# Layer 1's mixing and projection in one stage

## What is computed

```python
# layer 1, v = _gn(x); x becomes x + relu(res + out)
x_ft = rfft2(v) / sqrt(M * N)
a = x_ft[:, :, :32, :32]
blk1 = einsum('bixy,ioxy->boxy', a, fw1)      # complex, weights differ per mode
blk2 = einsum('bixy,ioxy->boxy', a, fw2)
out_ft[:, :, :32, :32] = blk1
out_ft[:, :, 256 - 32:, :32] = blk2           # row 224 + x of the output is k = -(32 - x)
out = irfft2(out_ft) / sqrt(N * (M // 2 + 1))
res = out @ W + b                             # 64 x 64
```

## Time and profile before

| | us |
|---|---|
| median of 3 runs | 2291.03 |
| lowest and highest run | 2281.13, 2308.48 |
| profiled execution, first to last instruction | 2287.4 |
| TensorE busy in it | 1824.6 |
| VectorE, ScalarE, GpSimd busy | 1462.2, 1128.0, 263.8 |
| mean granted TensorE clock | 0.876 of full speed |
| moved by DMA | 585.68 MB, 256 GB/s |

### The profile page before, as it was taken

One profiled execution on the slowest core, in us unless ns is written; L12 is line 12 of the kernel. 1 busy time (PEld: TensorE's weight loads), 2 busy tenths in 40 slices (PEclk: granted clock), 3 DMA queues, 4 the chain that ended last, 5 costly groups with the idle time before them and its releaser, 6 DMA issues. The chain is left out here.

```text
span 2287.4 us, 57711 instructions
## 1 busy us (share of the span) xinstructions
PE 1824.6 (80%) x24234; PEld 1460.3 (64%) x24234; DVE 1462.2 (64%) x2219; ACT 1128.0 (49%) x1852; POOL 263.8 (12%) x476
## 2 busy tenths in 40 slices
PE   5899989998197433332564999999989999999999
PEld 3677767677155333332553788787868878787887
DVE  5876777773447211112563788787868878787887
ACT  5765556662043000000333677676656767666665
POOL 0000000000102100000252110303021030303000
PEclk9999999999555556655876999999999999999999
DMA  8887887881965999996744888888887888888886
GB/s 302 311 262 239 260 267 255 264 270 23 219 77 110 265 253 284 254 264 172 237 150 133 295 282 289 305 311 321 298 299 271 284 321 296 320 311 319 296 293 261
DMA packets 240450, 585.68 MB, mean 256 GB/s; under 512 B 71170, under 2 KB 160770, under 8 KB 203906
## 3 DMA queue, kind: packets, MB, share of 16 engines
q1 hardware_dynamic: 163778, 515.47, 68.9%
q10 hardware_dynamic: 71040, 60.70, 10.4%
q0 software_dynamic: 5376, 5.76, 0.9%
HBM read 381.01 MB, written 168.30 MB: 240 GB/s over the span
## 5 line engine op out<-in xcount | busy, mean ns | idle before, releaser
L1298 ACT ACTIVATE x_turned<-ps_xt 128x512 f16<-128x512 f32 x512 | 305.6, 597 | 333.2 <-PE ps_xt L1384 333.2
L1428 PE MATMUL ps_y<-apply,x_turned 128*128 128x128 f16 x6144 | 428.5, 220 | 0.0
L1340 DVE TENSOR_TENSOR x_turned<-ps_xt,x_turned 128x512 f16<-128x512 f32 x512 | 351.2, 686 | 106.9 <-ACT x_turned L1298 106.9
L1428 PEld LDWEIGHTS ps_y<-apply,x_turned 128*128 128x128 f16 x6144 | 377.9, 98 | 64.8 <-issue 1.1
L221 DVE TENSOR_TENSOR parts<-stage,parts 128x1024 f16<-128x1024 f32 x256 | 301.9, 1220 | 107.7 <-ACT parts L145 107.1
L1361 DVE SCALAR_TENSOR_TENSOR y_out<-ps_y,relu 128x512 f32<-128x512 f32 x512 | 351.3, 686 | 22.6 <-PE ps_y L1428 4.1
L1384 PE MATMUL ps_xt<-c_eye,x_in 128*128 128x128 f32 x2048 | 312.2, 275 | 22.1 <-DMA x_in<-in_x 22.1
L1308 ACT ACTIVATE relu<-ps_wave 128x512 f32<-128x512 f32 x512 | 303.2, 592 | 13.8 <-PE ps_wave L1414 13.8
L145 ACT ACTIVATE parts<-stage 128x1024 f16<-128x1024 f32 x256 | 255.1, 1049 | 76.3 <-issue 40.7
L1332 DVE SCALAR_TENSOR_TENSOR low_tile<-ps_col,high_tile 128x512 f16<-128x512 f32 x256 | 176.6, 691 | 115.8 <-ACT high_tile L1292 115.8
L290 PE MATMUL row_ps<-parts,c_rows_dft 128*64 128x512 f16 x1536 | 200.6, 389 | 61.5 <-DVE parts L221 53.8
(11 more groups left out here) (121 smaller groups left out, 1978.7 us busy)
## 6 DMA issues: line engine op xcount, KB each, us to landing
stage<-in_x SPq DMA_DIRECT2D x256, 512.0 KB, 4.7
x_in<-in_x SPq DMA_DIRECT2D x128, 1024.0 KB, 9.6
out_y<-y_out SPq DMA_DIRECT2D x128, 1024.0 KB, 6.0
fw_first<-in_fw SPq DMA_DIRECT2D x9, 2048.0 KB, 19.5
fw<-in_fw ACTq DMA_DIRECT2D x8, 2048.0 KB, 22.8
fw<-in_fw SPq DMA_DIRECT2D x8, 2048.0 KB, 20.3
fw_first<-in_fw ACTq DMA_DIRECT2D x7, 2048.0 KB, 20.8
raw<-mixed ACTq DMA_DIRECT2D x12, 1024.0 KB, 7.4
```

What stands on the lines that cost most here:

```text
L1298: nc.scalar.activation(turned[u % 2][:, 0, :, :], ps_turn[u % 2][:, :, :], ACT.Copy).then_inc(turn_high, 1)
L1340: nc.vector.tensor_tensor(v[:, 1, :, :], ps_turn[u % 2][:, :, :], v[:, 0, :, :], ALU.subtract).then_inc(turn_split, 1)
L1428: mm = nc.tensor.matmul(ps_y[u % 2][:, :, 2 * k:2 * k + 2], turned[u % 2][:, p, k, :], apply[:, bass.ds(b, 1), q, :, :].rearrange("p o c w ...
```

## The change

`mixing_1` and `project_1` become one stage, `mix_project`, and `mixed` in memory goes. `norm_0` writes layer 1's modes into `x1`, even rows x in partitions 0 to 63 and odd rows in 64 to 127. fw1 is taken upwards as before, fw2 downwards (`x_of`): the chunk that mixes rows 4c to 4c + 3 of fw1 mixes rows 28 - 4c to 31 - 4c of fw2, which are k = -(4c + 1) to -(4c + 4). So both terms of a k are at hand when its projection comes.

Behind the second pass's step of a row, VectorE's copy (`mixed`, now a tile on the chip) is turned by eight transposes (`turn`), ScalarE copies them out in two pieces (`take_turn`), and `project` multiplies both terms of a k by a table made of W + 1 with the signs of the parts: for each half of the batch four fp32 products (two f, two parts) with 128 stationary columns and 256 moving ones; k = 0 and k = 32 have one f only. ScalarE writes the high part (`take_high`), VectorE the low part (`take_low`). Every eight k the rows are stored to `planes_1`, four DMAs of 256 KiB on SP and four on ScalarE (`store`); this happens in the third step of every second chunk. TensorE's list takes, in each step, projections first, then a turn, then the mixing step. `mixing_1` ran a loop of two chunks; the new lists are written out in full.

The planes of layer 0 and layer 1 are in two arrays now, so an image's planes come in two loads. Image 0's are loaded at the start of `pass_2`, and VectorE and ScalarE relay them in four parts each, between the first column groups, in place of GpSimd during `project_1`. `prepare` goes; VectorE builds the table at the start of `mix_project`. Cut to what is spoken of:

```diff
+def norm_0(nc, B, gram, apply, modes_x, planes_d, x1, fw, fw_first, w):
 ...
-        S_real = m.sb("S_real", [C, 2, K0, B, K0])
+        S_weighted, S_real = (x1[0:C, i * B // 2:(i + 1) * B // 2, :, :, :].rearrange("p b x r y -> p (b x r y)")
+                              .rearrange("p (r x b y) -> p r x b y", r=2, x=K0, b=B) for i in range(2))
 ...
                     for b in range(1, B, 2):
-                        v = xm[0:C, b, :, :, :].rearrange("p x r y -> p (x r y)")
-                        nc.scalar.activation(v, v, ACT.Copy, scale=rstd[0:C, b:b + 1]).then_inc(x1_ready[1], 1)
+                        for odd in range(2):
+                            nc.scalar.activation(x1[odd * C:(odd + 1) * C, b, :, :, :].rearrange("p x r y -> p x (r y)"),
+                                                 xm[0:C, b, odd::2, :, :].rearrange("p x r y -> p x (r y)"), ACT.Copy,
+                                                 scale=rstd[0:C, b:b + 1]).then_inc(x1_ready[1], 1)
 ...
             for b in range(0, B, 2):
-                v = xm[0:C, b, :, :, :].rearrange("p x r y -> p (x r y)")
-                nc.vector.tensor_scalar(v, v, rstd[0:C, b:b + 1], None, ALU.mult).then_inc(x1_ready[0], 1)
+                for odd in range(2):
+                    nc.vector.tensor_scalar(x1[odd * C:(odd + 1) * C, b, :, :, :].rearrange("p x r y -> p x (r y)"),
+                                            xm[0:C, b, odd::2, :, :].rearrange("p x r y -> p x (r y)"), rstd[0:C, b:b + 1],
+                                            None, ALU.mult).then_inc(x1_ready[0], 1)
 ...
+
+    def x_of(f, slot):
+        chunk, k = divmod(slot, KC)
+        return slot if f == 0 else K1 - KC - chunk * KC + k
+
+    def slot_of(f, k):
+        if f == 0:
+            return k
+        chunk = (k - 1) // KC
+        return chunk * KC + chunk * KC + KC - k
+
+    def terms(k):
+        return [f for f in range(2) if f == 0 and k < K1 or f == 1 and k > 0]
+
+    def turn_at(step):
+        chunk, s = divmod(step - KC - 1, CHUNK_STEPS)
+        return chunk * KC + s if 0 <= chunk < CHUNKS_1 and s < KC else None
+
+    def project_at(step):
+
+        chunk, s = divmod(step - KC - 2, CHUNK_STEPS)
+        if not 0 <= chunk < CHUNKS_1:
+            return []
+        return [k for k, at in ((chunk * KC, 0), (chunk * KC + 2, 2), (chunk * KC + 1, 3), (chunk * KC + 3, 4),
+                                (K1 if chunk == CHUNKS_1 - 1 else None, 4)) if at == s and k is not None]
+
+    order = [k for step in range(STEPS + 8) for k in project_at(step)]
 ...
+        weights = [fw_first] + [m.sb(f"fw{i}", [P, OH, KC, 2 * K1]) for i in range(1, SL)]
+        blocks = [m.sb(f"blocks{i}", [P, 2, 2, B, K1]) for i in range(KC)]
+        mixed = [m.sb(f"mixed{i}", [P, MG, 2, C]) for i in range(KC)]
+        T = [m.sb(f"mix_turned{i}", [P, 2, 2, B, K1]) for i in range(KC + 1)]
+        out = [m.sb(f"project_out{i}", [P, 2, 2, 2, 2, FLUSH, C], F16) for i in range(2)]
+        table = m.sb("project_table", [P, 2, 2, 2, 2, C])
 ...
+        def store(eng, blk, h, signal):
+            eng.wait_ge(out_high, rows_done(blk))
+            eng.wait_ge(out_low, rows_done(blk))
+            rows, places = row_pieces(blk, h)
+            for q in range(2):
+                for bh in range(2):
+                    eng.dma_start(planes_1[bh, :, q, :, rows, :].rearrange("p g k c -> p g (k c)"),
+                                  out[blk % 2][:, q, bh, :, h, places, :].rearrange("p g k c -> p g (k c)")
+                                  ).then_inc(signal[blk % 2], 16)
 ...
+            for step in range(STEPS + 8):
+                for blk in flush_at(step):
+                    store(sp, blk, 0, stored)
+                if step % KC == KC - 1 and step // KC + SL < LOADS:
+                    load(sp, 0, step // KC + SL)
 ...
+                        before = slot - KC if slot % KC else slot - 2 * KC
+                        if before >= 0:
+                            act.wait_ge(out_ready, max(number[k] for k in range(K1 + 1) for f in terms(k)
+                                                       if slot_of(f, k) == before) + 1)
+                    y0 = i * MG // 2
+                    nc.scalar.activation(
+                        turned(slot)[:, :, :, :, :].rearrange("p f r b (j g) -> p (f r b) j g", g=MG)[:, :, :, y0:y0 + MG // 2],
+                        ps_turn[i][:, :, :].rearrange("p g (j n) -> p n j g", j=4), ACT.Copy).then_inc(turn_taken, 1)
 ...
+                act.wait_ge(out_ready, number[k] + 1)
+                nc.scalar.activation(out[blk % 2][:, 0, :, :, :, at, :].rearrange("p n g h c -> p (n g h) c"),
+                                     ps_out[number[k] % 2][:, :, :, :, :].rearrange("p n g h c -> p (n g h) c"), ACT.Copy,
+                                     scale=PROJECT_SCALE).then_inc(out_high, 1)
 ...
+            for step in range(STEPS + 8):
+                for k in project_at(step):
+                    take_high(k)
+                for blk in flush_at(step):
+                    store(act, blk, 1, stored_sin)
+                slot = turn_at(step)
+                if slot is not None:
+                    take_turn(slot)
+                if step % KC == KC - 1 and step // KC + SL < LOADS:
+                    load(act, 1, step // KC + SL)
 ...
+            def take_low(k):
+                blk, at = divmod(k, FLUSH)
+                dve.wait_ge(out_high, number[k] + 1)
+                nc.vector.scalar_tensor_tensor(out=out[blk % 2][:, 1, :, :, :, at, :].rearrange("p n g h c -> p (n g h) c"),
+                                               in0=ps_out[number[k] % 2][:, :, :, :, :].rearrange("p n g h c -> p (n g h) c"),
+                                               scalar=PROJECT_SCALE,
+                                               in1=out[blk % 2][:, 0, :, :, :, at, :].rearrange("p n g h c -> p (n g h) c"),
+                                               op0=ALU.mult, op1=ALU.subtract).then_inc(out_low, 1)
+
 ...
+                if part == 0 and chunk >= 1:
+                    dve.wait_ge(turn_ready, 2 * ((chunk - 1) * KC + k + 1))
+                dve.wait_ge(ready, step + 1)
+                nc.vector.tensor_copy(mixed[k][:, :, :, part * OH:(part + 1) * OH].rearrange("p g w o -> p (g w) o"),
+                                      ps[step % BANKS][:, :, :, :].rearrange("p g w o -> p (g w) o")).then_inc(taken, 1)
+                if part == PASSES - 1 and chunk + 1 < CHUNKS_1:
+                    place((chunk + 1) * KC + k)
 ...
+            for step in range(STEPS + 8):
+                for k in project_at(step):
+                    take_low(k)
+                if step < STEPS:
+                    take_mixed(step)
 ...
+                for g in range(MG):
+                    for j in range(4):
+                        y = MG * j + g
+                        last = nc.tensor.matmul(ps[step % BANKS][32 * j:32 * j + R, g, :, :].rearrange("p w o -> p o w"),
+                                                blocks[k][:, :, :, :, y].rearrange("p f r b -> p (f r b)"),
+                                                weights[n % SL][:, :, k, 2 * y:2 * y + 2],
+                                                start=True, stop=True, tile_position=(0, 32 * j))
+                last.then_inc(ready, 1)
 ...
+                chunk, k = divmod(slot, KC)
+                pe.wait_ge(taken, chunk * CHUNK_STEPS + KC + k + 1 + BANKS)
+                for i in range(2):
+                    if slot >= 1:
+                        pe.wait_ge(turn_taken, 2 * (slot - 1) + i + 1)
+                    for g in range(MG // 2):
+                        last = nc.tensor.transpose(ps_turn[i][:, g, :],
+                                                   mixed[k][:, i * MG // 2 + g, :, :].rearrange("p w o -> p (w o)"), w["eye"][:, :])
+                    last.then_inc(turn_ready, 1)
+
+            def project(k):
+                n = number[k]
+                for f in terms(k):
+                    pe.wait_ge(turn_taken, 2 * (slot_of(f, k) + 1))
 ...
+                    pe.wait_ge(out_low, n - 1)
+                for bh in range(2):
+                    pairs = [(f, r) for f in terms(k) for r in range(2)]
+                    for f, r in pairs:
+                        last = nc.tensor.matmul(
+                            ps_out[n % 2][:, bh, :, :, :].rearrange("p g h c -> p (g h c)"),
+                            turned(slot_of(f, k))[:, f, r, bh * HB:(bh + 1) * HB, :].rearrange("p b y -> p (b y)"),
+                            table[:, f, r, :, :, :].rearrange("p g h c -> p (g h c)"), start=((f, r) == pairs[0]),
+                            stop=((f, r) == pairs[-1] and k > 0))
 ...
+            for step in range(STEPS + 8):
+                for k in project_at(step):
+                    project(k)
+                slot = turn_at(step)
+                if slot is not None:
+                    turn(slot)
+                if step < STEPS:
+                    mix(step)
 ...
```

(100 more changed lines are left out.)

440 lines of the change are left out of this document (112 added, 328 removed).

## The result

| | before | changed | forecast |
|---|---|---|---|
| median of 20 runs each (us) | 2290.4 | 2302.3 | 2153 |
| ratio to before, 95% interval | | 1.005 (1.003 to 1.007) | 0.94 |
| span of the profiled execution | 2287.4 | 2305.7 | 2149.8 |
| first column of the last pass starts | 1213.36 | 1103.55 | 1068.7 |
| last pass's first wave product | 1244.0 | 1141.7 | |

The change made the kernel half a per cent slower. The first column comes 110 us earlier, and the last pass, which the change left alone in my sum, gives 121 us back; its column phase takes 7.5 us more, near the forecast (+7). Windows of the changed kernel, columns as in the earlier trace rows: the mixing stage, the stretch between it and the first column, the last pass.

A forecast was written before the change was run, and what follows sets the result against it. The last pass was taken as TensorE's own and unchanged; mixing waited on uneven loads, project_1 left engines idle. First column 144.6 us earlier, less 7 for relay pairs: net -137.6, span 2149.8, plus 3.6 gives 2153 us; 8-in-10 range 2105 to 2225.

The forecast's parts named there:

- forecast (+7): Last pass, first 16 column groups: three more pairs of relay parts, 7 us added (4 to 13).
- step 8: Before the last pass: image 0's planes load with nothing beside them, two issues and 7.5 us, together 8, to 1066.4.
- C: Rival: in mixing, load halves run one after the other, 21 us each, 46 us a chunk, 2223; chance 0.13.
- Steps 1 to 4: Start of mixing: block starts at 747, next load at 761.8 after the first pass, chunk 0 done at 777.8.
- Step 5: Mixing stage: seven chunks of 36 us each, ending at 1029.8.
- Step 7: Between mixing and last pass: last stores and block change take 14 us, to 1058.4.
- Step 9: Before the first column: VectorE and ScalarE each turn a part of image 0, 2.3 us, first column at 1068.7.
- E: Rival: strided results double a warm mixing step, 1.05 to 2.1 us, 44.4 us a chunk, 2216; chance 0.06.
- The rule of the Trainium skill that I weighed: Mixing results: non-contiguous PSUM patterns slow matmuls significantly; the forecast still left the mixing step at 1.05 us.
- three stalls of a second pass: In each chunk's second pass, TensorE waits about 1 us for copies: twice before a turn, once before a projection.
- D: Rival: TensorE bounds mixing at half clock, 53.6 to 55.6 us a chunk, 2294 to 2308; chance 0.07.
- A: Main forecast: TensorE paces the mixing stage, mostly warm, 33 to 40 us a chunk, 2132 to 2181; chance 0.62.

The follow-up runs named there:

- version with four loads: The changed kernel with each planes_1 load of 4 times 32 rows issued as four loads of 32 rows: 2180.8 us, ratio 0.952.
- later clearing: On the kernel with four planes loads of 32 rows, GpSimd clears the second tile_0 only after VectorE's first turn of image 0: 2177.4 us, ratio 0.949.

## Why the prediction was wrong

**The step that failed** is step 8, "Image 0's planes are now loaded with nothing beside them: two issues and 7.5 us", and with it the sentence "Later images' planes come in two loads instead of one and land within 17.7 us, under an image of 130 us (1043 / 8)." With that sentence fell the premise that the last pass, TensorE's own, stays as it was. I took the landing from the old load, which had another form, and never asked what form the new one has. I also asked only whether the planes are in time. GpSimd has an image for them; the `x_in` load queued behind them has not. I had named what stands behind ScalarE's stores, and did not name what stands behind this load. It cost 22.5 us at step 8 (30.5 for 8) and 112.5 us in the last pass (134.6 - 22.1), and 8 more by TensorE's lower clock around the stops (1024 busy for 1016; from 1372 to 1376, behind one, the granted clock is 0.50). That is 143 of the 156 us by which the profiled span missed (2305.7 for 2149.8); 10 more are a start of the block 10 us late, which is told below. No rival named it; C was about slow loads of `fw`. The rule of the Trainium skill quoted above (*DMA: Bandwidth & Descriptors*) speaks of just this form.

**The steps that held.** In the version with four loads, whose mixing stage is the same:

- *Steps 1 to 4:* the block's first load goes out at 746.8 (forecast 747), the next at 762.75 (761.8), the one after chunk 0 at 781.3 (777.8).
- *Step 5:* from 781.26 to 1002.75 six chunks, 36.9 us each for 36. The last copy ends at 1051.2 for 1044.4.
- *Step 7:* the planes' issue came at 1060.3 for 1058.4, but by luck: from the last copy it took 9.1 us where I had 14, which hid 5 of the 7 us lost before.
- *Step 8, with the load's form mended:* 8.2 us for 8.
- *Step 9:* 1068.96 with the later clearing, forecast 1068.7. Without it 1075.29: a collision that I had not looked for.

Even so the version with the later clearing took 2177.4 for 2153: its `x_in` stops are 36.6 us for 22.1, and TensorE is busy for 1027.5 us in the last pass for 1016, at clock 0.98.

In the changed kernel's own profile the block starts 10 us later, at 757. That is not the change: the 128 column products at the end of the first pass, code that the change doesn't touch, ran there at clock 0.58 (552 to 566) and 0.50 (566 to 577), in the version with four loads at 1.00. Changed kernel and version with four loads:

```profile
551.82 25.33 PE L334 MATMUL mode_ps<-c_cols_dft,rows_turned 128*128 128x64 f32 x128 [0.83 <-issue]
```

```profile
L334 PE MATMUL mode_ps<-c_cols_dft,rows_turned 128*128 128x64 f32 x128 | 14.5, 275 | 0.8 <-issue 0.8
```

**The prices.** One pass in the changed kernel's timeline:

```profile
924.61 3.72 PE L1076 MATMUL project_ps<-project_table,mix_turned 128*128 128x256 f32 x16
...
928.17 1.04 PE L1061 MATMUL mix_turn_ps<-c_eye,mixed 128*128 128x128 f32 x8
...
929.13 1.29 PE L1048 MATMUL mix_ps<-fw,blocks 128*32 128x64 f32 x64
...
931.24 1.09 PE L1061 MATMUL mix_turn_ps<-c_eye,mixed 128*128 128x128 f32 x8 [0.81 <-DVE mixed L999]
```

A projection takes 3.56 us to the next instruction (forecast 3.45), a turn 0.96 (1.22). The 64 mixing products take 1.29 us with the end of the last, whose median is 0.23, so 1.06 from the first start to the last (forecast 1.05). The strided results cost nothing here (1.06 for 1.04 to 1.05), and E falls. The rule of the Trainium skill that I weighed (*PSUM — Partial Sum Buffer*, section Specifications) is not what this product shows. Of the three stalls of a second pass the two ahead of turns are 0.8 us each for 1 (16 in the stage, 12.9 us); the one ahead of a projection came once in the whole stage. D falls with a clock of 0.94.

**Right for partly the wrong reason:** A said that TensorE paces the stage. Both halves of a load go out together, as forecast (934.97 on both queues), but land after 16.6 to 20.9 us at the median, not 12 to 14, near C's 21: the 349 GB/s was that of a window of 4 us, and the whole stage moved 230. Taking 43 us of work from TensorE gave 21 back, so loads and TensorE both pace it. I read the 36 us as two passes of 15 us with their waits and two loads of 17 to 20, which happen to end together; that reading is argued, not shown.

## What to carry to other kernels

When a change alters how data lies in memory, read the form of every load that fetches it, its outermost dimension above all, and not only its bytes and its count: padding one row, or a layout that suits the store, cost 120 to 200 us here. A transfer that has time itself may still be late for what queues behind it or shares its engines, so price it by the next thing that lands. A stop of TensorE can cost more than its length, by the lower clock behind it. Where a stage improves and the total doesn't, compare the waits of the stages that the change was not about.

## What the runs showed that I had not expected

- A load on four engines delays one on sixteen even from another queue: `x_in` 33 to 35 us from ScalarE-issued planes, 13 to 16 with the planes on all engines.
- From the first issue to the landing, image 0's planes took 8.2 us with four loads of 32, 19.2 alone with one load of outermost 4, 30.5 with that beside `x_in`, and 34.1 with two loads of outermost 2. Time doesn't go as one over the engines.
- GpSimd's clearing stretched a group of four of VectorE's 16-bit copies from 1.37 to 6.54 us, GpSimd's copies beside it to 2.61 and 3.66.
- The clock at the end of the first pass fell to 0.50 in the profile of the changed kernel and 10.9 us went with it; of the others here only the run with `x_in` behind its planes shows products that slow (up to 423 ns for 275). What decides it stays open.
